# Row-maximum products on 64 rows into two PSUM banks, one maximum over both, and swapped banks for the gate and up projections

## The reference

```python
q = (x @ Wq.T).reshape(b, t, N_HEADS, HEAD_DIM)          # 8 heads of 64
kv_latent = x @ Wkv_down.T                               # 64 numbers per token
k = (kv_latent @ Wk_up.T).reshape(b, t, N_HEADS, HEAD_DIM)
v = (kv_latent @ Wv_up.T).reshape(b, t, N_HEADS, HEAD_DIM)
scores = jnp.einsum('bqhd,bkhd->bhqk', q, k) * HEAD_DIM ** (-0.5)
out = jnp.einsum('bhqk,bkhd->bqhd', jax.nn.softmax(scores, axis=-1), v)
attention = out.reshape(b, t, N_HEADS * HEAD_DIM) @ Wo.T

gate = fp4_linear(x, w_gate)                             # both operands on a 4-bit grid,
y = fp4_linear(x, w_up)                                  # one scale for every 16 numbers
feed_forward = fp4_linear(jax.nn.silu(gate) * y, w_down) # hidden width 704
```

## Time and profile before

| | |
|---|---|
| median of three runs | 1498.85 us |
| the profiled execution's own time | 1497.88 us |
| its span, first to last instruction | 1496.1 us |
| mean granted TensorE clock | 0.984 of full speed |
| instructions | 25492 |
| PE matmuls, VectorE, GpSimd, ScalarE busy | 93%, 80%, 81%, 48% of the span |

### The profile page before, as it was taken

The page is one execution under the profiler, slowest core; times in us unless marked ns, Lnnn a source line. Parts: engine busy times, 40 slices in busy tenths (PEclk is TensorE's granted clock), DMA queues, the critical chain, the costliest instruction groups (busy, mean ns, idle before and its releaser), DMA issues.

```text
span 1496.1 us, 25492 instructions
## 1 busy us (share of the span) xinstructions
PE 1383.9 (93%) x7910; PEld 1021.1 (68%) x7910; DVE 1189.6 (80%) x2472; ACT 716.9 (48%) x1574; POOL 1213.7 (81%) x1336
## 2 busy tenths in 40 slices
PE   1489999999999999999999999999999999999996
PEld 1356677776767777676777677677767767676675
DVE  7677978888787888878888887888888788867662
ACT  3444545445454544545454454545454554545441
POOL 7648888879788887978888788879878887986773
PEclk9689999999999999999999999999999999999998
DMA  4032222222223222222222222222212322221220
GB/s 125 0 78 56 62 79 69 61 65 71 72 58 78 71 65 58 72 75 60 72 72 67 55 72 79 64 65 72 74 50 70 82 63 62 65 68 49 59 58 29
DMA packets 73557, 98.07 MB, mean 66 GB/s; under 512 B 12752, under 2 KB 40144, under 8 KB 73424
## 3 DMA queue, kind: packets, MB, share of 16 engines
q1 hardware_dynamic: 73424, 96.45, 24.4%
HBM read 37.16 MB, written 8.65 MB: 31 GB/s over the span
## 4 chain that ended last, share of the span: by engine, by line
PE 63%; DVE 17%; POOL 11%; issue 4%; ACT 3%; DMA 1%; SPq 0%; POOLq 0%; DVEq 0%; ACTq 0%
PE m L871 30%; PE po L1032 12%; PE mx L971 5%; PE st L999 5%; PE st L1000 5%; POOL key_sum L518 4%; DVE row_max L723 4%; PE m L1046 2%; DVE inv_den L794 2%; DVE hid L768 2%; DVE hid L764 2%; DVE xn L819 1%; PE m L1124 1%; PE m L983 1%; POOL h_norm L537 1%
## 5 line engine op out<-in xcount | busy, mean ns | idle before, releaser
L608 ACT ACTIVATE probs<-st 128x512 f32<-128x512 f32 x512 | 284.0, 594 | 334.3 <-PE st L1000 334.3
L518 POOL TENSOR_TENSOR key_sum<-key_sum,probs 128x512 f32<-128x512 f32 x256 | 329.1, 1285 | 38.0 <-ACT probs L608 1.7
L723 DVE TENSOR_REDUCE row_max<-mx 128x1 f32<-128x512 f32 x512 | 322.9, 672 | 1.2 <-PE mx L971 0.6
L1032 PE MATMUL po<-probs,lat_tok 128*64 128x512 f32 x1024 | 233.8, 598 | 0.0
L999 PE MATMUL st<-q_hi,lat 128*128 128x512 f32 x512 | 216.9, 424 | 0.5 <-ACT probs L608 0.5
L1000 PE MATMUL st<-q_lo,lat 65*128 65x512 f32 x512 | 203.1, 397 | 0.0
L971 PE MATMUL mx<-lat,q_hi 128*128 128x512 f32 x512 | 176.0, 418 | 11.4 <-DVE row_max L723 4.3
L871 PE MATMUL m<-wgu_hi,xt_hi 128*128 128x352 f32 x512 | 168.8, 330 | 3.5 <-DVE lat_tok L851 1.7
L616 ACT ACTIVATE hid<-m 128x352 f32<-128x352 f32 x128 | 59.5, 465 | 233.7 <-PE m L871 233.7
L871 PE MATMUL m<-wgu_hi,xt_lo 128*128 128x352 f32 x512 | 166.3, 325 | 0.0
L871 PE MATMUL m<-wgu_lo,xt_hi 128*128 128x352 f32 x512 | 166.1, 324 | 0.0
(11 more groups left out here) (179 smaller groups left out, 3347.4 us busy)
## 6 DMA issues: line engine op xcount, KB each, us to landing
q_hi<-qp_hi SPq DMA_DIRECT2D x256, 128.0 KB, 2.3
q_lo<-qp_lo SPq DMA_DIRECT2D x128, 128.0 KB, 2.4
inv_b<-inv_rows SPq DMA_DIRECT2D x128, 128.0 KB, 2.8
x_in<-in_L_attn_x_dram SPq DMA_DIRECT2D x64, 128.0 KB, 2.3
acc<-in_L_attn_x_dram SPq DMA_DIRECT2D x64, 128.0 KB, 2.1
out_dram<-acc SPq DMA_DIRECT2D x32, 256.0 KB, 2.9
q_lo<-neg_max SPq DMA_DIRECT2D x128, 2.0 KB
inv_rows<-inv_den SPq DMA_DIRECT2D x64, 4.0 KB
```

The source lines that it names most:

```text
L518: pool.tensor_tensor(total, first, last, ALU.add).then_inc(sum_step, 1)
L608: act.activation(probs[:, t.c % 2, kc, :], st[kc % 2][:, :], ACT.Exp).then_inc(exp_done, 1)
L723: dve.tensor_reduce(row_max[:, u.c % 2, qc:qc + 1], mx[qc % 2][:, :], AX.X, ALU.max).then_inc(mx_taken, 1)
L1032: last = pe.matmul(po[v * R:(v + 1) * R, :], lat_tok[:, s.c % 2, kc, 0:R], probs[:, v, kc, :], start=(kc == 0), stop=(kc == CH - 1))
```

## The change

Each pair of `query_scores` becomes one call with two matmuls. Each has 64 rows of contraction: the first takes rows 0 to 63 of `q_hi` for one query block against the high part of the latent in `lat`, the second rows 64 to 127 of `q_hi` for the next query block against the same high part in rows 64 to 127 of `lat1`. They write the two banks of one PSUM tensor `mx`. The low part of the latent no longer enters the maxima. VectorE takes both maxima with one `tensor_reduce`, and the pair waits for the whole reduce before it.

To make room for this, `lat1` and `q_lo` grow to 128 rows with the data in rows 64 to 127, the row of ones and the negated maximum in row 0, and zeros in rows 1 to 63; L1000's contraction grows from 65 to 128 rows. The wait for the latent's low part moves from `query_scores` to `key_scores`, and the low part waits for both ScalarE copies.

`gate` goes into `m1` and `up` into `m0`. So the query projection waits for `silu_done` and the down projection for `hid_done`. `up` goes first in slots 5 and 7 (after the latent and its transposes, which use `m1`) and no longer in slots 3 and 4.

```diff
-        mx = [psum("mx0"), psum("mx1")]
+        mx = ctx.enter_context(nc.psum_tensor("mx", [P, 2, 512], F32))
...
-            def max_rows(t, qc):
+            def max_rows(t, half):
                 u = t.plus(2)
                 if u.within(SLOTS):
-                    dve.wait_ge(mx_psum, u.n(CH, qc + 1))
-                    dve.tensor_reduce(row_max[:, u.c % 2, qc:qc + 1], mx[qc % 2][:, :], AX.X, ALU.max).then_inc(mx_taken, 1)
+                    dve.wait_ge(mx_psum, u.n(CH, 2 * half + 2))
+                    dve.tensor_reduce(row_max[:, u.c % 2, 2 * half:2 * half + 2], mx[:, :, :], AX.X, ALU.max).then_inc(mx_taken, 1)
...
-                    act.activation(lat1[0:R, s.c % 2, :], m1[0:R, :], ACT.Copy).then_inc(lat_hi_done, 1)
+                    act.activation(lat1[R:P, s.c % 2, :], m1[R:P, :], ACT.Copy).then_inc(lat_hi_done, 1)
...
-                    dve.wait_ge(lat_hi_done, s.n(2, 1))
+                    dve.wait_ge(lat_hi_done, s.n(2, 2))
...
-            dve.memset(lat1[R:R + 1, :, :].bitcast(F32), 1.0).then_inc(ones_ready, 1)
+            dve.memset(lat1[0:R, :, :].bitcast(F32), 0.0).then_inc(ones_ready, 1)
+            dve.memset(q_lo[0:R, :, :].bitcast(F32), 0.0).then_inc(ones_ready, 1)
+            dve.wait_ge(ones_ready, 2)
+            dve.memset(lat1[0:1, :, :].bitcast(F32), 1.0).then_inc(ones_ready, 1)
...
-                    if qc == 0:
+                    if half == 0:
                         pe.wait_ge(q_hi_placed[u.c % 2], m.n(2 * 16, 2 * 16))
                         pe.wait_ge(lat_hi_done, s.n(2, 2))
-                        pe.wait_ge(lat_lo_done, s.n(1, 1))
-                    if u.any(CH, qc - 1):
-                        pe.wait_ge(mx_taken, u.n(CH, qc - 1))
-                    pe.matmul(mx[qc % 2][:, :], q_hi[:, u.c % QH, qc * P:(qc + 1) * P], lat[:, s.c % 2, :],
-                              start=True, stop=True).then_inc(mx_psum, 1)
+                    if u.any(2, half):
+                        pe.wait_ge(mx_taken, u.n(2, half))
+                    for v, keys in enumerate((lat, lat1)):
+                        rows, qc = slice(v * R, (v + 1) * R), 2 * half + v
+                        pe.matmul(mx[:, v, :], q_hi[rows, h, qc * P:(qc + 1) * P], keys[rows, s.c % 2, :],
+                                  start=True, stop=True).then_inc(mx_psum, 1)
...
             def gate(t):
 
                 if t.within(SLOTS):
+                    m1_free(t.plus(-1))
+                    into_hidden(t, m1, 0, gate_psum)
+
+            def up(t):
+
+                if t.within(SLOTS):
                     m0_free(t.plus(-1))
-                    into_hidden(t, m0, 0, gate_psum)
-
-            def up(t):
-
-                if t.within(SLOTS):
-                    m1_free(t.plus(-1))
-                    into_hidden(t, m1, I, up_psum)
+                    into_hidden(t, m0, I, up_psum)
...
                 query_scores(t, 0)
-                query_scores(t, 1)
-                if wov_half(t.plus(-1)) is None:
+                if lat_seq(t.plus(-1)) is None and ltok_seq(t.plus(-1)) is None:
                     gate(t)
                     up(t)
                 else:
...
-                        pe.wait_ge(hid_done, t.n(1, 1))
+                        pe.wait_ge(silu_done, t.n(1, 1))
```

44 lines of the change are left out of this document (22 added, 22 removed).

## The result

| | before | after |
|---|---|---|
| median of the runs | 1498.86 us (1497.68 to 1499.71, 8 runs) | 1503.20 us (1502.17 to 1504.41, 8 runs) |
| span of the profiled execution | 1496.1 us | 1501.9 us |
| mean granted TensorE clock | 0.984 | 0.982 |
| instructions of VectorE | 2472 | 2218 |

The ratio is 1.003, with a 95% interval from 1.0019 to 1.0041: the kernel became slightly slower. The forecast was 1502 us and "slower" was the likeliest of the three. The number came out right, but, as the last sections show, partly by luck: two errors of opposite sign met.

What follows compares the result with a forecast made beforehand. TensorE was taken to bound the stretches behind query projections, VectorE's work those ahead: +0.96 − 0.65 = +0.31 us a sequence, +5.0 in 16, +0.4 at the start, on 1497.88: 1503.3, stated as 1502. Range 1476 to 1526.

Steps and rivals of the forecast that it cites:

- The mechanism of the pair: Maxima products on TensorE: mode switch drains both ways, bare loads, two matmuls side by side; +0.12 us per pair.
- rival 2: Drain comes, but the pair is not side by side: serial loads 1521 us, serial matmuls too 1544; chance 0.10.
- rival 1: 64-row mode costs no drain between fp32r matmuls, pair takes 0.235 us; -3.7 us a sequence, 1439 us; chance 0.16.
- Behind the query projections: TensorE is the bound there and meets two pairs per odd-even stretch: 4 × 2 × 0.12 = +0.96 us a sequence.
- Elsewhere the reduce is over in time: Outside slot 1, the pair's wait for the whole merged reduce costs nothing; in slot 1 `gate` starts +0.15 us.
- Slot 3: Query projection starts 0.85 us earlier: `gate` goes first, tanh ends earlier, and two pair penalties are subtracted.
- Slot 7: Query projection starts 0.05 us later, with `gate` now the projection that waits for the latent's transposes.
- Slot 5: Query projection starts 0.47 us later: L830 waits for L667's end, `gate` for L830, then tanh and L764.
- Slot 1: VectorE-bound; query projection 0.67 us earlier in the sequence read, less 0.35 for average waits: mean gain 0.32.
- The lead-in: Two added VectorE fills at the start, at most 4.0 us, mostly hidden by a 2.78 us token-chunk wait: +0.4.
- The sum: +0.96 behind and -0.65 at the query projections' starts: +0.31 us a sequence, +5.0 in 16; with start, 1503.3 us.
- Rival 3: `gate`'s wait in slot 5 pushes VectorE's queue back; half a microsecond more a sequence, 1510 us; 0.02 beyond main range.

Runs made afterwards that it cites:

- same rows: The changed kernel with both matmuls of a pair on the same rows 64 to 127, so they can't run side by side; 1552.08 us, ratio 1.0362.
- full rows: The changed kernel with the two maxima products over all 128 rows as before, keeping shared buffer, single reduce and bank swap; 1493.88 us, ratio 0.9975.
- swap alone: The kernel before with only the banks of `gate` and `up` exchanged and the order that goes with it; 1478.12 us, ratio 0.9873.
- Low part early: The changed kernel with ScalarE copying rows 64 to 127 first and VectorE subtracting right after that copy; 1496.57 us, ratio 0.999.
- pair alone: The changed kernel with the banks, order and waits of `gate` and `up` as before; 1526.90 us, ratio 1.0195.
- mixed banks: The bank swap without the pair, but with the old banks in slots 5 and 7, `gate` first in every slot; 1476.76 us, ratio 0.9859.

## Why the prediction was right, and where it was not

**The mechanism of the pair: right.** Drain, two row groups in parallel, a bare load on each side. The records are 3 ns apart, which rules out rival 2, and "same rows" shows what rival 2 would have looked like. The penalty is 0.14 and not negative, which rules out rival 1. The term was slightly too small, 0.14 against 0.12; around slot 3, "full rows" gives back 0.14 to 0.16 a pair.

**Behind the query projections: +0.96 forecast, +0.90 measured.** Right in size, but not wholly for the reason given. The sum took eight pairs at the switch's price, against a kernel before in which nothing else waits. But there the second matmul of the first pair of slots 2, 6 and 0 started 0.08 late behind its block's reduce, and that much of the switch's price had been paid already. And I had written "Elsewhere the reduce is over in time", checked for slot 1 only. In slots 2, 6 and 0 it is, but by 0.04 to 0.05 us; in slot 7 the pair starts 0.15 behind the reduce, like one that waits for it. "Full rows" shows what this means: without any switch the stretches behind slots 1, 5 and 7 are as long, because the end of the merged reduce is then the limit.

**Slot 3: −0.85 forecast, −0.76 measured. Slot 7: +0.05 and +0.06.** Right; "swap alone" gives 1.01 for slot 3 without the pairs' penalties, of which the forecast had subtracted two.

**Slot 5: +0.47 forecast, +0.62 measured.** Mechanism right: L830 waits for ScalarE's second copy, `gate` waits for L830, and the tanh and L765 follow. "Low part early" takes exactly this away, 0.62. The forecast chained the single durations of the earlier trace rows; the place in the trace after is 844.64 with its wait of 0.20 for L765, as described. Its loss was booked under the swap of the banks, though: the swap alone loses nothing there (8.18), and "pair alone" without the swap as much (8.92). It is the second copy.

**Slot 1: −0.32 forecast, −0.78 measured.** Here a step failed. I spread the total of the waits over the slots, found that the query projection of slot 1 waits 0.35 less on average than in the sequence that I had read, and took that off the gain of 0.67. But the stretch ahead of slot 1 is 7.55 to 7.72 in 11 of 14 sequences before, and 6.79 to 6.80 in all after. In four of these 11 the query projection waited only 0.13 or 0.14 us, because TensorE had already waited 0.78 to 0.81 at the products of the maxima. A wait that is missing at one instruction had been paid at another; only three sequences were really shorter (7.02 to 7.35). Without the correction the forecast would have been −0.67. The gain was forecast too small by 0.46 us a sequence, or 7 us in 16, and 0.35 of the 0.46 are this step.

**The lead-in: +0.4 forecast, +5.2 measured.** I counted on the 2.78 us wait for the second token chunk to hide the fills. It did not, because the fills stand ahead of the first chunk's statistics, not in that wait. The two new fills took 2.7 us (the 0.91 of the ones had been there before), and with the gaps between them the statistics start 3.2 us later. I did not price the pairs of the last lead-in slots at all, nor time at the lower clock. Moving the fills took 3.1 us off in the traces, with a difference in the granted clock in it; how the other 2 us divide is open.

**The sum.** Steady state +0.31 a sequence forecast, +0.10 measured: 3.4 us too high. Lead-in 4.8 us too low. They cancel to within 1.4 us, of which the tail, which the sum did not have, took back 0.9. That is why the sum of 1503.3 met the 1503.7 us of the profiled execution (its span of 1501.9 and 1.8 around it), and it is luck. The step from there to 1502, for drains that fall into waits, is not borne out by a number of its own. The forecast of 1.19 for the reduce and of a nearly unchanged busy share of TensorE held. Rival 3, a queue of VectorE pushed back for slots, did not come: the stretch ahead of slot 7 grew by 0.06 only.

**What beats both.** Swap alone (1478.1 us) and mixed banks (1476.8 us) are both below the kernel before, by 1.3% and 1.4%, with overlapping intervals. The best form here is the swap without the pair; which of the two is better is not told apart. Every kernel with the shared buffer, the best of them at 1485.1 us, stays above the swap alone.

## What to carry to other kernels

Price a change in pieces, and each piece stretch by stretch: this one held a gain of 19 us and a loss of 29, and its result near zero told neither. A single pair on two row groups loses 0.14 us here, although running side by side saves it 0.23, because the way in and the way out cost more. A second pair right behind the first would save its 0.23 without a switch of its own and so come out ahead; that is an estimate from these numbers, no run here has two in a row. And before an average of waits is used, the stretch between two fixed points should be measured in several sequences: a wait can move to another instruction and look as if it were gone.
